# Long cross-attention on one core: weighted sums for four key tiles at a time, from sixteen buffers of exponentials

## What is computed

```python
def _L3_xattn_ref(query, key, value, Wq, Wk, Wv, Wo):
    H, HK = (16, 4); HD = 8; G = 4
    q = (query @ Wq).reshape(b, qlen, H, HD)
    k = (key @ Wk).reshape(b, kvlen, HK, HD)
    v = (value @ Wv).reshape(b, kvlen, HK, HD)
    qg = q.reshape(b, qlen, HK, G, HD)
    scores = jnp.einsum('bqkgd,bskd->bkgqs', qg, k) / sqrt(HD)
    attn = jax.nn.softmax(scores, axis=-1)
    out = jnp.einsum('bkgqs,bskd->bqkgd', attn, v)
    return out.reshape(b, qlen, H * HD) @ Wo
```

## Time and profile before

| | |
|---|---|
| median of 3 runs | 1134.63 us (1134.15 to 1136.45) |
| the profiled execution: its own time | 1134.68 us |
| the profiled execution: span from first to last instruction | 1132.6 us |
| mean granted TensorE clock over the span | 0.854 |
| the long attention's two passes | from about 857 us to 1102 us of the span |

### The profile page before, as it was taken

One profiled execution on the slowest core, in us unless ns is written; L12 is line 12 of the kernel. 1 busy time (PEld: TensorE's weight loads), 2 busy tenths in 40 slices (PEclk: granted clock), 3 DMA queues, 4 the chain that ended last, 5 costly groups with the idle time before them and its releaser, 6 DMA issues. The chain is left out here.

```text
span 1132.6 us, 18246 instructions
## 1 busy us (share of the span) xinstructions
PE 909.4 (80%) x6163; PEld 563.6 (50%) x6163; DVE 737.3 (65%) x2038; ACT 588.4 (52%) x1774; POOL 242.1 (21%) x354
## 2 busy tenths in 40 slices
PE   5887999999697263569776799894778999999986
PEld 2346899999455131425543377483662233333323
DVE  6456677777465597355486644714557889888823
ACT  5584677777333100313354434642352777777773
POOL 4002455555200122202111000332501111111100
PEclk8698999999798686658886899786795999999997
DMA  9600000000002600000001000561112111110000
GB/s 235 157 2 1 1 2 1 1 2 2 1 0 32 85 0 14 16 0 1 1 1 53 1 1 1 167 169 46 23 38 65 22 22 24 25 25 9 2 1 14
DMA packets 76174, 35.81 MB, mean 32 GB/s; under 512 B 35226, under 2 KB 74561, under 8 KB 76082
## 3 DMA queue, kind: packets, MB, share of 16 engines
q1 hardware_dynamic: 73714, 33.61, 13.4%
q0 software_dynamic: 896, 0.63, 0.2%
q10 hardware_dynamic: 1472, 0.41, 0.2%
HBM read 24.42 MB, written 11.05 MB: 31 GB/s over the span
## 5 line engine op out<-in xcount | busy, mean ns | idle before, releaser
L527 ACT ACTIVATE L3x_E<-L3x_pS 128x400 f32<-128x400 f32 (+1 forms) x384 | 167.8, 507 | 48.0 <-PE L3x_pS L621 47.1
L443 DVE TENSOR_REDUCE L3x_NMP<-L3x_pM 128x1 f32<-128x361 f32 x384 | 178.1, 525 | 18.2 <-PE L3x_pM L599 17.2
L599 PE MATMUL L3x_pM<-ctx_tm 64*128 64x361 bf16 x384 | 103.8, 339 | 14.3 <-DVE L3x_NMP L443 9.5
L621 PE MATMUL L3x_pS<-ctx_tm 64*128 64x400 bf16 (+1 forms) x384 | 107.0, 348 | 3.4 <-ACT L3x_E L527 2.1
L1540 ACT ACTIVATE L0x_E<-L0x_E,ctx_r 128x100 f32<-128x100 f32 x288 | 105.1, 369 | 2.0 <-DVE L0x_E L1428 1.9
L599 PEld LDWEIGHTS L3x_pM<-ctx_tm 64*128 64x128 bf16 x384 | 30.3, 96 | 109.8 <-DVE L3x_NMP L443 90.2
L636 PE MATMUL L3x_pO<-L3x_E,CT 128*32 128x400 f32 (+1 forms) x768 | 84.8, 514 | 0.0
L1643 PE MATMUL L0x_pS<-L0x_QS,CT 128*128 128x100 f32 x576 | 71.0, 282 | 1.3 <-ACT L0x_QS L1532 1.3
L1357 POOL TENSOR_TENSOR L0x_E<-L0x_E,L0x_RZ 128x1200 f32<-128x1200 f32 x24 | 52.6, 2192 | 80.8 <-DVE L0x_RZ L1448 80.8
L1643 PEld LDWEIGHTS L0x_pS<-L0x_QS,CT 128*128 128x128 f32 x576 | 69.0, 199 | 1.5 <-ACT L0x_QS L1532 1.5
L1655 PE MATMUL L0x_pU<-ctx_tm,L0x_E 128*100 128x129 f32 x576 | 67.9, 273 | 1.7 <-POOL L0x_E L1357 1.1
(11 more groups left out here) (647 smaller groups left out, 2126.1 us busy)
## 6 DMA issues: line engine op xcount, KB each, us to landing
ctx_tm<-in_ctx SPq DMA_DIRECT2D x8, 704.0 KB
ctx_tm<-key_terms SPq DMA_DIRECT2D x16, 270.8 KB, 4.3
key_terms<-ctx_tm SPq DMA_DIRECT2D x42, 90.2 KB
ctx_tm<-in_L_ffn_wi SPq DMA_DIRECT2D x4, 512.0 KB, 8.0
ctx_tm<-in_L_ffn_wo SPq DMA_DIRECT2D x4, 512.0 KB, 8.2
ctx_tm<-query_terms SPq DMA_DIRECT2D x16, 75.0 KB, 3.5
slots_in<-L2a_zeros SPq DMA_DIRECT2D x8, 129.0 KB
L2f_XS<-slots_in SPq DMA_DIRECT2D x4, 258.0 KB, 3.2
```

The lines of the kernel that those rows point to most:

```text
L443: nc.vector.tensor_reduce(NMP[:, p, i // NC4, a, i % NC4:i % NC4 + 1], v, AX.X, ALU.max, negate=True).then_inc(s_mr, 1)
L527: nc.scalar.activation(E[0:r, n % EB, :], pS[0:r, n % 3, 0:NG * T], ACT.Exp, scale=SCALE8).then_inc(s_e, 1)
L599: nc.tensor.matmul(pM[:, n % 3, 0:CW], key_rows(QS, a)[:, b, p, 128 * x:128 * x + 128], key_rows(KS, a)[:, b % KB, c, p, :], start=True, s ...
L621: nc.tensor.matmul(pS[0:NW[k], n % 3, 0:NG * T], key_rows(KS, a)[:, b % KB, k % 4, p, 128 * (k // 4):128 * (k // 4) + NW[k]], key_rows(QS, ...
```

## The change

`weigh` takes four key tiles at a time in place of two, so eight matmuls in a row in place of four; two key tiles share each quarter of the accumulator. There are three such groups in a unit in place of six, in steps start(u) + 5, 9 and 13. The buffers of exponentials are sixteen in place of eight, and the two waits are rewritten for the new counts. Everything else stands.

```diff
-    EB = 8
+    EB = 16
+    WG = 4
+    WEIGH_AT = 5
...
         def group_step(t):
             for u in range(NU):
-                r = t - start(u) - 3
-                if 0 <= r < NKT and r % 2 == 0:
-                    return u, r // 2
+                r = t - start(u) - WEIGH_AT
+                if 0 <= r < NKT and r % WG == 0:
+                    return u, r // WG
             return None
...
                             v, kk = (n - EB) // 24, (n - EB) % 24 // 2
-                            act.wait_ge(s_pv, 4 * (6 * v + kk // 2 + 1))
+                            act.wait_ge(s_pv, 24 * v + 2 * WG * (kk // WG + 1))
...
                 def weigh(u, g):
                     b, p = u // 2, u % 2
-                    pe.wait_ge(s_e, 24 * u + 4 * g + 4)
+                    pe.wait_ge(s_e, 24 * u + 2 * WG * (g + 1))
                     if g == 0 and p == 0 and b >= 1:
                         pe.wait_ge(s_oc, b)
-                    for x in range(2):
-                        k = 2 * g + x
+                    for x in range(WG):
+                        k = WG * g + x
                         for a in range(2):
                             n = 24 * u + 2 * k + a
-                            r = 32 * (2 * x + a)
+                            r = 32 * (2 * (x % 2) + a)
                             nc.tensor.matmul(pO[r:r + 32, 0:NG * T], V[0:NW[k], b, k, a, 16 * p:16 * p + 32],
-                                             E[0:NW[k], n % EB, :], start=(p == 0 and g == 0),
-                                             stop=(p == 1 and g == 5), skip_group_check=True).then_inc(s_pv, 1)
+                                             E[0:NW[k], n % EB, :], start=(p == 0 and g == 0 and x < 2),
+                                             stop=(p == 1 and k >= NKT - 2), skip_group_check=True).then_inc(s_pv, 1)
```

## The result

The changed kernel takes 1165.72 us (median of 4 runs, 1164.85 to 1168.08) where the one before takes 1134.39 (4 runs, 1133.73 to 1136.45): 1.0276 times as long, 95% interval 1.0256 to 1.0296, or +31.3 us. Forecast were 1161.0, that is +26.3, and a range from 1152 to 1168.

The account below looks back on a forecast made before the run. VectorE, pacing maximum tiles through three banks and running dry after bursts, was taken as what bounds the kernel. Seven batches +24.1, beginning -0.8 and tail +3.0 gave +26.3 on 1134.68, so 1161.0 us; range 1152 to 1168.

Parts of the forecast that it names:

- The bound: Long attention: VectorE paces maximum tiles through three banks and runs dry once in two steps, losing 0.30 us.
- The length of a burst: Weighted sums: two more matmul waves add 0.72 us, so the next maximum tile comes 1.53 after the start.
- Where it is paid: Per batch, six kept bursts pay 0.72 each, 4.32; three removed return 0.95, three nothing: +3.37 us.
- every removed burst returns its 0.30: Rival for the removed bursts' gaps: a kept burst costs only 0.42, giving 1154 us; chance 0.15.
- The chain of maxima: Step 16's copy of maxima, GpSimd addition and step 20's score shift later: 0.0 to 0.2 a batch, taken 0.1.
- The beginning: The removed first burst, step 23, returns 0.8 us; about +0.6 instead if step 25's burst meets half clock.
- The clock: Stage granted 1.00 throughout; the rival has half clock for most of it, +60, 1220 us, chance 0.03.
- the tail: From step 208 ScalarE sets the pace: six kept bursts +4.3, removed gaps -1.4; +3.0 us taken.
- the seven batches: From the burst in step 25 to that in step 207: 7 x 3.45 = +24.1 us.
- a clock that leaves 1.00: Sign in the profile after that the prediction would be wrong: the granted clock not staying at 1.00.
- bursts with a seam: Rival for the long burst: 1.62 in place of 1.53 for 48 bursts, +4.5, so 1165.5 us; chance 0.15.
- The buffers: Sixteen buffers of exponentials and rewritten waits: cost and gain nothing, as the wait for a free buffer never held anything.

Follow-up runs that it names:

- e3_half_work: The changed kernel without the weighted sums of each group's third and fourth key tile, leaving bursts of four in the same steps: 1133.09 us, 0.9995 of before.
- e2_adjacent: The changed kernel with each burst of eight matmuls cut into two of four at the ends of adjacent steps: 1142.03 us, 1.0080 of before.
- e1_buffers: The changed kernel with weighted sums for two key tiles at a time as before, keeping only the sixteen buffers: 1133.24 us, 0.9989 of before.

## Why the prediction was right, and where it was off

*The bound.* Right. VectorE paces the maximum tiles through three banks and runs dry after a burst. e3_half_work shows both sides: whole bursts taken out of the batch, 4.9 of TensorE's time, return 0.95, so TensorE's total does not set it; the second halves of long bursts, 4.02 of its time, return 4.02, so the length of the burst does. e2_adjacent agrees, with the place of half of the matmuls changed as well.

*The length of a burst.* The mechanism holds, the size was off: the two further waves took 0.67 and not 0.72, since the four waves start 0.36, 0.34 and 0.33 apart (961.95, 962.31, 962.65 and 962.98 in one burst) and sixteen records end after 1.55. Six times 0.05 is 0.3 of the 3.45 a batch.

*Where it is paid.* Right. Kept bursts 6 x 0.67, three gaps returned, three not: 4.02 - 0.95 = 3.07, and the undisturbed batch is 3.07 longer. By the gaps themselves the six pay 4.05: the burst of step 25 paid 0.58 and not 0.67, as the small operations of lines 455 and 456 still filled 0.09, and that of step 20 paid 0.78. In e3_half_work the 0.95 stands alone. That makes the rival "every removed burst returns its 0.30" wrong. The gaps themselves were to be 0.9 to 1.0 and are 0.58 to 1.27, because those of before were not all 0.22 but 0 to 0.60.

*The chain of maxima.* I put 0.1 on it. The gap after step 16 grew by 1.27 - 0.60 = 0.67, as any other, and the next one by 1.05 - 0.27 = 0.78, which leaves 0.1 for it. That the chain is what took this 0.1 was not tested by itself.

*The beginning.* -0.7 against -0.8 up to the burst of step 25. That burst met the half clock, the case for which the text had named about +0.6 in all, and its 1.2 lie in the next stretch, in its 28.0: -0.7 + 1.2 = +0.5.

*The clock.* The step that failed. The prediction took 1.00 for the whole stage; its rival let the clock fall for most of the stage (+60) and had 0.03. What happened lies between: the first burst in the half clock (1.2), four falls among the maximum tiles (5.3) and one in the tail (1.1), 7.6 together. With 3.07 x 7 = 21.5, -0.7, 2.6 in the tail without its fall and 0.6 outside, the 31.6 are accounted for. The error of 5.3 us is this term (+7.6), the overestimate of the seven batches (-2.7) and of the tail (-0.4), and what lies outside the stage (+0.6). The prediction had named a clock that leaves 1.00 as a sign that it is wrong, and in this term it is.

*The luck.* 1165.7 lies outside the 1161 within 3 that had the chance of 0.58, and inside the range only because of its upper part. That part was there for bursts with a seam, forecast at 1165.5, and the time came out at almost that number. But there is no seam: the burst took 1.48 and not 1.62. The clock, which had no part in the range beyond the beginning, filled the room made for the seam, and without its 7.6 the time would have been about 1158. The slowdown and its mechanism were foreseen; that the error is 5.3 and not 7.6 is two errors of opposite sign.

*The buffers.* Right: nothing (e1_buffers), and in the changed kernel no exponential waited for a weighted sum.

*What is open.* Why a fall comes in one batch and not in the next, which has the same pattern, is not settled, nor why one run with the copies had a lower clock than all others. Nor was the number of banks itself varied: three are the maximum tiles', three the scores', and I did not take one from the other.

## What to carry to other kernels

When one engine alternates between feeding others through a few buffers and a longer job of its own, compare the length of the job with what the buffers hold; merging jobs to save switches is paid on the side that was fed, and the whole lengthening shows once the stock was already used up. Before counting what a removed burst returns, look whether other operations were filling its gap, and before moving a burst, what stands beside it. A forecast of a change that makes TensorE wait more needs a term for its clock. A cut job is worth its second entry only where a gap stood and nothing else did, and buffers have to be counted anew for every cut.

## What the runs showed of the hardware that was not expected

The granted TensorE clock fell to 0.50 for some 3.5 us at a time in the middle of a stage in which TensorE shows 27.78 us busy of 31.70, after steps in which it waited a little before the tiles (7.31 busy of the 8.70 before one fall, from 958.2 to 966.9). With waits filled by useless matmuls it held 1.00 for 218 us in the profiled execution. Leaving out half of the weighted sums brought falls as well: the undisturbed batch got 0.95 shorter and the median did not.

Four matmul waves on the four column quarters started 0.36, 0.34 and 0.33 apart: sixteen records took 1.55 in one burst, but 1.76 as two bursts of eight, of which the second had to wait for the last exponentials.
